# A decoder layer on one core: channels of x regrouped by partition, opening loads on two queues, first rounded chunk taken from PSUM

## The reference

```python
Xn = _layernorm(X, gamma, beta)
QKV = Xn @ W_in + b_in
Q, K, V = jnp.split(QKV, 3, axis=-1)
K = _rotary(K, ROT_DIM)
V = _rotary(V, ROT_DIM)
A = jnp.sum(_cos_sim(K) * _cos_sim(V), axis=-2)
A = (1.0 - IDENTITY_WEIGHT) * A + IDENTITY_WEIGHT
Y = A[:, None, :] * Q
Y = Y @ W_out + b_out
return Y + X
```

## Time and profile before

| | |
|---|---|
| median of 3 runs | 791.81 us (791.77 to 791.91) |
| span of the profiled execution | 789.7 us, 10694 instructions (its own device time is not recorded; the median is 2.1 us above its span) |
| TensorE busy | 774.6 us, 98% of the span, granted clock 0.997 of full speed |
| VectorE, ScalarE, GpSimd busy | 663.4, 322.7, 357.4 us |

### The profile page before, as it was taken

The page is one execution under the profiler, slowest core; times in us unless marked ns, Lnnn a source line. Parts: engine busy times, 40 slices in busy tenths (PEclk is TensorE's granted clock), DMA queues, the critical chain, the costliest instruction groups (busy, mean ns, idle before and its releaser), DMA issues.

```text
span 789.7 us, 10694 instructions
## 1 busy us (share of the span) xinstructions
PE 774.6 (98%) x3590; PEld 637.1 (81%) x3590; DVE 663.4 (84%) x1346; ACT 322.7 (41%) x704; POOL 357.4 (45%) x308
## 2 busy tenths in 40 slices
PE   8999999999899999999999999999999999999996
PEld 7888888887667778888888888888888888888885
DVE  6888679998898870476779998999999999899875
ACT  6444336456574422222443433334333343343314
POOL 1241222242122411014476676776776677676323
PEclk9999999999999999999999999999999999999998
DMA  8666504624454528001122231431333224242013
GB/s 321 249 131 164 94 5 101 169 79 76 79 143 110 158 84 289 1 1 32 60 70 79 82 89 40 127 95 46 93 114 106 87 79 119 60 132 55 16 63 150
DMA packets 51046, 79.92 MB, mean 101 GB/s; under 512 B 17487, under 2 KB 26447, under 8 KB 50480
## 3 DMA queue, kind: packets, MB, share of 16 engines
q0 software_dynamic: 24240, 31.52, 18.6%
q1 hardware_dynamic: 25168, 47.72, 17.2%
q10 hardware_dynamic: 1584, 0.01, 0.1%
HBM read 110.64 MB, written 12.58 MB: 156 GB/s over the span
## 4 chain that ended last, share of the span: by engine, by line
PE 64%; DVE 4%; issue 2%; POOL 2%; ACT 1%; POOLq 0%; DVEq 0%; ACTq 0%
PE gu L1870 14%; PE gu L1871 14%; PE gu L1869 14%; PE ob L1947 6%; PE ob L1943 6%; PE ob L1942 6%; DVE scratch L1566 1%; DVE scratch L1568 1%; POOL h_lo L1306 1%; DVE x_lo L1613 1%; PE gu L2041 0%; PE ob L1896 0%; ACT junk L1443 0%; DVE xall L1607 0%; PE ob L1963 0%
## 5 line engine op out<-in xcount | busy, mean ns | idle before, releaser
L1869 PE MATMUL gu<-x_hi,w_hi 128*128 128x512 f32 x516 | 201.4, 390 | 0.0
L1871 PE MATMUL gu<-x_hi,w_lo 128*128 128x512 f32 x516 | 200.8, 389 | 0.0
L1870 PE MATMUL gu<-x_lo,w_hi 128*128 128x512 f32 x516 | 200.7, 389 | 0.0
L1306 POOL TENSOR_TENSOR h_lo<-mid,h_hi 128x512 fp32r<-128x512 f32 x62 | 86.8, 1417 | 176.0 <-ACT h_hi L1455 176.0
L1871 PEld LDWEIGHTS gu<-x_hi,w_lo 128*128 128x128 f32 x516 | 96.8, 188 | 20.1
L1869 PEld LDWEIGHTS gu<-x_hi,w_hi 128*128 128x128 f32 x516 | 96.9, 188 | 20.1
L1870 PEld LDWEIGHTS gu<-x_lo,w_hi 128*128 128x128 f32 x516 | 96.9, 188 | 19.9
L1465 ACT ACTIVATE gates<-dots 128x1 f32<-128x1 f32 x144 | 29.2, 203 | 175.3 <-DVE dots L1715 175.3
L1624 DVE TENSOR_TENSOR mid<-gu,mid 128x512 f32<-128x512 f32 x64 | 44.0, 687 | 66.4 <-PE gu L1871 56.5
L1942 PE MATMUL ob<-w_hi,h_hi 128*128 128x512 f32 x224 | 87.1, 389 | 0.0
L1943 PE MATMUL ob<-w_lo,h_hi 128*128 128x512 f32 x224 | 87.1, 389 | 0.0
(11 more groups left out here) (254 smaller groups left out, 1431.0 us busy)
## 6 DMA issues: line engine op xcount, KB each, us to landing
stage<-in_ctx SPq DMA_DIRECT2D x7, 1024.0 KB, 5.6
total<-prod POOLq DMA_DIRECT2D x11, 384.0 KB, 4.3
xall<-half_bo POOLq DMA_DIRECT2D x4, 1024.0 KB, 9.2
xhat<-in_L_ffn_gate_w SPq DMA_DIRECT2D x8, 512.0 KB, 3.5
xhat<-in_L_ffn_up_w SPq DMA_DIRECT2D x8, 512.0 KB, 3.7
xall<-in_mask_Bx1xS_ff POOLq DMA_DIRECT2D x4, 1024.0 KB, 10.4
xhat<-in_L_ffn_down_w SPq DMA_DIRECT2D x8, 512.0 KB, 3.6
x_dram<-xall SPq DMA_DIRECT2D x4, 1024.0 KB, 6.7
```

Source lines behind the costliest of these rows:

```text
L1306: nc.gpsimd.tensor_tensor(lo[:, c], mid[c][:], hi[:, c].bitcast(F32), ALU.subtract).then_inc(hlo_done, 1)
L1869: nc.tensor.matmul(dst, lhs[0], rhs[0], start=start, stop=False)
L1870: nc.tensor.matmul(dst, lhs[0], rhs[1], start=False, stop=False)
L1871: return nc.tensor.matmul(dst, lhs[1], rhs[0], start=False, stop=stop)
```

## The change

A partition now holds four neighbouring channels: chunk c, partition p is channel 4p + c. The rows of W_in are loaded in that order, xhat is written in that order from an x read with a step of four elements, and gamma and beta load as 128 pieces of 16 bytes each. Tile 0 of x stays on SP's queue; tile 1, ident, gamma and beta are issued on ScalarE's; b_q moves to SP's queue behind x of batch 1. For chunk 0 of part 0, ScalarE writes xn_hi directly from PSUM, and VectorE computes xs from PSUM, after waits for gamma and beta and for `hi_done`, in front of w_lo of chunk 0. `scaled_x` on ScalarE has one more wait (`xs_done`), met in order.

```diff
-    w_in_v = w_in.rearrange("(c p) n -> c p n", p=P)
+    w_in_v = w_in.rearrange("(p c) n -> c p n", c=KC)
...
-                sp.dma_start(xall[:, 0:2 * D], x_tiles[0][:, 0]).then_inc(x_half, 16)
-                sp.dma_start(ident[:], consts[:, C_ID:C_ID + P]).then_inc(ident_in, 16)
+                sp.dma_start(xall[:, 0:D], x_tiles[0][:, 0, 0:D]).then_inc(x_tile[0], 16)
...
-                sp.dma_start(qT[:], w_in.rearrange("(c p) n -> p c n", p=P)[:, :, 0:D]).then_inc(wq_raw, 16)
+                sp.dma_start(qT[:], w_in.rearrange("(p c) n -> p c n", c=KC)[:, :, 0:D]).then_inc(wq_raw, 16)
                 load_x(1)
+                sp.dma_start(b_q[:], b_in[0:D].rearrange("(c p) -> p c", p=P), allow_slow_non_contiguous=True).then_inc(bq_in, 16)
...
-                for dst, src, count in ((gam, gamma, gb_in), (bet, beta, gb_in), (b_q, b_in[0:D], bq_in)):
-                    act.dma_start(dst[:], src.rearrange("(c p) -> p c", p=P), allow_slow_non_contiguous=True).then_inc(count, 16)
+                act.dma_start(xall[:, D:2 * D], x_tiles[0][:, 0, D:2 * D]).then_inc(x_tile[1], 16)
+                act.dma_start(ident[:], consts[:, C_ID:C_ID + P]).then_inc(ident_in, 16)
+                for dst, src in ((gam, gamma), (bet, beta)):
+                    act.dma_start(dst[:], src.rearrange("(p c) -> p c", c=KC)).then_inc(gb_in, 16)
...
+                    act.wait_ge(xs_done, j)
                     nc.scalar.activation(xs[:, c % 2, part_cols(p)], x_bank(p, c)[:, part_cols(p)], ACT.Identity, scale=gam[:, c:c + 1], bias=bet[:, c:c + 1]).then_inc(xs_done, 1)
...
                 for c in range(KC):
-                    high(0, c)
+                    if c == 0:
+                        act.wait_ge(xt_mm, 1)
+                        nc.scalar.activation(xn_hi[:, 0, part_cols(0)], x_bank(0, 0)[:, part_cols(0)], ACT.Identity, scale=gam[:, 0:1], bias=bet[:, 0:1]).then_inc(hi_done, 1)
+                    else:
+                        high(0, c)
...
-                        nc.vector.tensor_scalar(xhat[:, i], tile(j), mv[:, j, 0:1], rstd[:, j:j + 1], ALU.subtract, ALU.mult).then_inc(xhat_done, 1)
+                        nc.vector.tensor_scalar(xhat[:, i].rearrange("p (c q) -> p c q", c=KC), tile(j).rearrange("p (q c) -> p c q", c=KC), mv[:, j, 0:1], rstd[:, j:j + 1],
+                                                ALU.subtract, ALU.mult).then_inc(xhat_done, 1)
...
-                dve.wait_ge(x_half, 16)
-                x_stats(0, (0, 1))
+                for i in range(2):
+                    dve.wait_ge(x_tile[i], 16)
+                    x_stats(0, (i,))
                 x_variance(0)
                 normalise(0)
+                dve.wait_ge(gb_in, 32)
+                dve.wait_ge(hi_done, 1)
+                nc.vector.tensor_scalar(xs[:, 0, part_cols(0)], x_bank(0, 0)[:, part_cols(0)], gam[:, 0:1], bet[:, 0:1], ALU.mult, ALU.add).then_inc(xs_done, 1)
                 low_w(0)
+                dve.wait_ge(xs_done, 1)
                 low(0, 0)
```

More of the change, by code:

```diff
@@ L200, in decoder_layer @@
             x_in = [sem(f"x_in{b}") for b in range(B)]
-            x_half = sem("x_half")
+            x_tile = [sem("x_tile0"), sem("x_tile1")]
             w_raw = [sem(f"w_raw{c}") for c in range(KC)]
```

## The result

| | before | after |
|---|---|---|
| median | 791.79 us (791.76 to 791.91, 4 runs) | **795.8 us** (795.71 to 796.1, 4 runs) |
| profiled execution: span | 789.7 us | 794.3 us (its own device time is 796.1) |
| TensorE, VectorE, ScalarE, GpSimd busy | 774.6, 663.4, 322.7, 357.4 us | 775.9, 666.6, 322.4, 359.5 us |

The ratio is 1.0049 (95% interval 1.0037 to 1.0061): slower by 4.0 us. Forecast were +1.8 us. The sign and the range held; the size was off by more than a factor of two.

The account below looks back on a forecast made before the run. VectorE's unbroken run was taken to set TensorE's chunk 1 at 13.09. VectorE's +0.92 and 1.08 for four xhat tiles make +2.0, less 0.24 gives 1.76; about +1.8 on 791.81 gives 793.6 us, range 791.9 to 796.2.

Parts of the forecast that it names:

- the 0.24: Before batch 1: ScalarE's instruction at 45.74 had waited 0.24 us for TensorE, taken off VectorE's +2.0 to give 1.76.
- xn_hi of chunk 0 at 8.3: Opening, ScalarE: input ready at about 8.3, once tile 1 is transposed, so the direct xn_hi is there at 8.85.
- +0.67: Opening, VectorE: w_lo of chunk 0 starts at 9.34 instead of 8.67, moving TensorE's chunk 1 from 13.09 to 13.76.
- The new xs instruction: Opening, VectorE: xs of chunk 0 from PSUM takes 542 ns, 0.46 us from start to start.
- The step: VectorE's xhat reading x with a 16-byte step: 809 ns instead of 542, +0.27 us a tile, bounds 0 and +0.80.
- Rival 1: VectorE's xhat: the step costs nothing, so the kernel is not measurably slower, 792.3 us; chance 0.28.
- rival 2: VectorE's xhat: a dearer step, 794.2 us at 0.37 a tile, 797.8 us at 0.80; chance 0.13.
- Gamma and beta, behind x and ident there, are needed at 8.3 only.: Opening, ScalarE's load queue: gamma and beta may stand last, since nothing needs them before 8.3; no cost counted.
- Iota: TensorE near 23: iota lands before 23.1, the 0.27 wait shrinks to 0.05, and TensorE goes from +0.67 to +0.45.
- Behind the opening: From the second half of batch 0 to batch 1: VectorE reaches +2.0, TensorE's start at 47.00 moves by 1.76.
- The sign given for it: TensorE at batch 1's start: a wait of about 1.8 us at 48.8 for xn_hi would show the forecast right.
- The remaining 8 xhat tiles lie under VectorE's own waits: Later batches: 2 x 1.08 us is hidden by VectorE's waits of 2.25 at 81.64 and 1.84 at 106.33.

Follow-up runs that it names:

- psum_first_only: before with only xn_hi of chunk 0 written directly from PSUM and its xs moved to VectorE; 792.76 us, ratio 1.0014.
- ident_on_sp: after with only the ident load moved back to SP's queue, behind tile 0 of x; 794.43 us, ratio 1.0038.
- one_queue: after with tile 1 of x and ident back on SP's queue in front of the weights, only gamma and beta on ScalarE's; 795.11 us, ratio 1.0038.
- no_step: after with xhat read and written contiguously, so the first products pair wrong channels but the work is the same; 794.2 us, ratio 1.0031.
- after_plain: after without the direct xn_hi and VectorE's new xs: ScalarE writes xs and xn_hi of chunk 0 as before; 794.25 us, ratio 1.0031.
- one_queue kernels: The three kernels one_queue, one_queue_plain and one_queue_pe_step; 795.11, 793.47 and 792.6 us.
- layout_only: before with only the channel grouping, strided xhat and 16-byte pieces for gamma and beta, all loads on their old queues; 793.59 us, ratio 1.002.
- layout_pe_step: layout_only with xhat contiguous and TensorE's transposes reading every fourth channel instead; 792.1 us, ratio 1.0005.
- one_queue_plain: one_queue without the direct xn_hi and VectorE's new xs; 793.47 us, ratio 1.0018.
- after_again: The unchanged kernel after, run and profiled a second time; 795.99 us, ratio 1.0049 against before.
- one_queue_pe_step: one_queue_plain with xhat contiguous and TensorE's transposes reading every fourth channel instead; 792.6 us, ratio 1.0006 against before.
- b_q_late: before with only the b_q load moved to SP's queue, behind x of batch 1; 792.29 us, ratio 0.9997.

## Why the prediction was right in sign and wrong in size

- **Bound, and the places read.** Right in the main: VectorE's run sets TensorE's chunk 1, and the sum on VectorE less the 0.24 gives the start of batch 1. Later stages were read too coarsely (see the last point).
- **xn_hi of chunk 0 at 8.3.** Wrong by 0.4. The prediction took the transposes as the only input and left out w_hi, in front of it on ScalarE and itself at 7.58 to 8.54; that is what sets 8.66 in psum_first_only. In ident_on_sp it is the transposes after all (8.69, a wait of 0.18 for them), since x came at 4.14 and not 3.8, and xhat ended at 8.21 and not 8.0. With 0.1 more on the way to xs, w_lo of chunk 0 goes to 9.78 and 9.83, not 9.34. The term "+0.67" measures +1.1.
- **The new xs instruction.** 542 ns forecast, 545 measured, 0.46 from start to start: right.
- **The step.** +0.27 forecast, +0.19 measured: mis-sized, in the lower half of the bounds. The estimate from the Trainium skill, "SBUF — State Buffer", section "Door 1: The DMA port swizzle", and "Vector Engine (DVE) Microarchitecture Reference", section 5.2, was 0.18 to 0.37; the measured 0.19 agrees with its low end. Rival 1 (no cost) and rival 2 are out.
- **"Gamma and beta, behind x and ident there, are needed at 8.3 only."** This is the step that failed. Being needed late was taken as arriving in time; the landing was not worked out. It is 9.9, and w_lo of chunk 1 is 1.0 to 1.3 us later than in ident_on_sp (13.96 and 14.25 against 12.97). At batch 1 the two profiles of after are 1.7 and 2.3 behind ident_on_sp; less the 0.44 of the clock in the one and the 0.77 of GpSimd in the other, beta's share is an estimated 1.3 to 1.5. The earlier trace rows and the sooner landing of loads were read as bytes per microsecond, and those did get better (x at 4.19 and not 3.8 or 4.33; weights 0.8 sooner). The Trainium skill's sentence, "DMA: Bandwidth & Descriptors", section "Issuing engines are not separate DMA queues", was used for bandwidth alone. It also says that loads of all issuers interleave, and with that this trace agrees: 86 pieces of one queue beside 86 of the other in a microsecond.
- **Iota.** Right that it holds nothing up: issued at 14.13, it lands 8.4 us later, at 22.5. Wrong that the gap would close to 0.05. The weight load at 25.19 stands 0.30 behind the product in front of it, now put down to issue, and in before it was 0.27. So TensorE did not go down from +0.67 to +0.45; in ident_on_sp it is at +1.15 at chunk 1 and at +1.19 behind the gap.
- **Behind the opening.** 1.76 at batch 1 was forecast (its own formula, 0.67 - 0.21 - 0.24 + 6 x 0.27, gives 1.84). ident_on_sp gives 1.83, one_queue 1.52. The agreement is luck in part: +0.45 at the start and -0.08 a tile for six tiles cancel. The sign given for it, a wait of about 1.8 us for xn_hi at 48.8, did not come: that wait is 0.44 in every kernel with a strided xhat, as it was 0.42 in before. TensorE takes the delay on in several places, +1.19 behind the iota gap, +1.4 where it waits for qT (at 40.47), +1.76 where the transposes wait for ScalarE's xs (at 47.73) and +1.83 at batch 1 in ident_on_sp; the rows at 42.45 and 50.02 show the same waits in after.
- **"The remaining 8 xhat tiles lie under VectorE's own waits."** Half right. The four of batch 2 do: from batch 1 to batch 2 nothing is added but 0.1. The four of batch 3 stand behind the wait of 1.84 at 106.33, not in front of it: +0.77.
- **The range.** 791.9 to 796.2 held, by luck: its upper part was there for a step dearer than 0.27 (rival 2), and the step was cheaper. Beta's landing, which filled it, was in no rival.

The sum, redone: 1.8 as forecast, 1.7 to 2.3 for beta (with the clock or GpSimd's wait, as above), 0.8 for the last four tiles, less 0.4 that batch 3 gives back in the profile of after (+5.00 at its start, +4.6 at its end). That is 3.9 to 4.5, against 4.0 in the medians and 4.6 between the two spans. What the change was worth in its parts, by the medians, each taken above before on its own chip: moving ident alone back to SP's queue saves 1.2 (ident_on_sp, +2.9 against +4.0), leaving out the step 1.7 (no_step, +2.3), leaving out the direct first chunk 1.6 to 1.7 (after_plain, +2.5). They don't add up to 4.0, since the delays of the opening overlap.

How far the account of beta's landing is shown: while both queues have work, they move equal numbers of pieces, and a load's own bytes don't matter (64 KB or 2 KB, both 128 pieces, at the same place). That they take turns piece by piece on each engine is argued from the counts; the order on one engine is in none of these views. Nor do these runs part the place on the queue from the instant of issue: the fourth load is always issued at 2.13. That the other queue's pieces set the pace fits two more pairs: beta as the second load, behind gamma alone and issued at 1.17, lands at 4.4 to 4.6 in the one_queue kernels, where x comes on SP's queue in pieces of 2 KB, and at 5.3 to 5.5 in layout_only and layout_pe_step, where they are 4 KB.

## What to carry to other kernels

A load that is "needed only later" needs a landing time of its own: its place on the queue, and how large the pieces are that the other queue moves meanwhile. A small operand that gates a whole chain goes on a queue by itself or to its head. Before taking a delay as hidden under an engine's wait, check in the order of time that the wait stands behind the delay, not before it, and that what it waits for doesn't move too. And a new instruction in front of work that needs less than it does gives away the time in which that work would have run for nothing.

## What was not expected of the hardware

- A load of 2 KB takes 2.8 to 3.4 us to land on a queue that holds only its like (one_queue), and 7.5 to 7.8 us as the fourth of its queue while SP's is full. Behind tile 1 of x, by place on ScalarE's queue, the landing on the clock is 5.3 to 7.0 for the second, 7.95 to 8.45 for the third and 9.6 to 9.9 for the fourth, for 64 KB of ident as for 2 KB. The two queues move equal numbers of pieces, 86 and 86 between 7 and 8 us of after, though one piece takes 0.17 us and the other 0.009.
- A one-source VectorE instruction of 512 fp32 columns that reads SBUF with a step of 16 bytes takes 735 ns instead of 540; the same step in TensorE's 128-column transposes costs 11 ns (284 against 273).
- GpSimd's rnorm of two columns takes 0.69 us in one execution and 2.83 in another (after, one_queue_plain), while the wgt behind it shrinks from 1.62 to 0.19; together 2.4 against 3.1 us. Within one_queue_plain the records of rnorm run from 0.70 to 2.85. Why is open, and times on GpSimd are rough.
- The granted clock falls to 0.50 for 2 to 3 us in the opening of three of the profiles (after_again, after_plain, one_queue_pe_step), after waits of TensorE of 1.2 to 1.9 us, and not in b_q_late behind 1.87, nor in after and no_step behind 1.24 and 1.60.
- The first weights land up to 1.1 us apart between profiles of kernels whose loads are issued alike (w_hi at 7.18, 7.72 and 8.26 in the three one_queue kernels; 6.16 to 6.82 in after, after_again, after_plain and no_step). With the same issues in front on SP's queue and different ones on ScalarE's it is 2 us (6.88 to 8.94). A difference under 1 us in the opening can't be read from one profile.
